# Attentions of a decoder layer: the product by the inverse one quarter earlier on VectorE, the layernorm scale behind a mask on GpSimd, the split of the output weights at a group's end

## The reference

```
x = x + attention(layernorm(x))                       # causal, 16 heads of 32
x = x + cross_attention(layernorm(x), ctx, ctx, mask) # keys and values of ctx, padding masked
x = x + experts(layernorm(x))                         # the one expert with the highest probability of 8
```

## Time and profile before

| | us |
|---|---|
| median of 3 runs | 2038.52 |
| lowest, highest | 2037.73, 2043.76 |
| profiled execution: its time | 2036.4 |
| profiled execution: its span | 2034.7 |

### The profile page before, as it was taken

The page is one execution under the profiler, slowest core; times in us unless marked ns, Lnnn a source line. Parts: engine busy times, 40 slices in busy tenths (PEclk is TensorE's granted clock), DMA queues, the critical chain, the costliest instruction groups (busy, mean ns, idle before and its releaser), DMA issues. The chain is left out here.

```text
span 2034.7 us, 34889 instructions
## 1 busy us (share of the span) xinstructions
PE 1882.0 (92%) x10942; PEld 1325.2 (65%) x10942; DVE 1342.8 (66%) x2837; ACT 1140.2 (56%) x2179; POOL 1000.9 (49%) x1147
## 2 busy tenths in 40 slices
PE   2999999999999999999999999999999835999997
PEld 2666666767666766656666666666666324898896
DVE  3666676666667676767575757575765335688886
ACT  3455554555555465655565655565655515787885
POOL 3354555455545555445444545555554434345454
PEclk9999999999999999999999999999999967899999
DMA  6444545545454575445454544535443369322220
GB/s 202 105 101 110 123 103 131 120 107 135 109 132 100 124 182 125 110 113 125 105 125 105 119 111 111 119 87 127 91 103 79 74 201 333 121 78 88 79 86 21
DMA packets 138089, 239.96 MB, mean 118 GB/s; under 512 B 31114, under 2 KB 32434, under 8 KB 137872
## 3 DMA queue, kind: packets, MB, share of 16 engines
q1 hardware_dynamic: 105728, 191.00, 34.7%
q0 software_dynamic: 21968, 46.42, 11.6%
q10 hardware_dynamic: 10240, 0.64, 0.3%
HBM read 115.63 MB, written 50.02 MB: 81 GB/s over the span
## 5 line engine op out<-in xcount | busy, mean ns | idle before, releaser
L535 ACT ACTIVATE attn_probs<-attn_sT 128x512 f32<-128x512 f32 (+3 forms) x1024 | 529.1, 519 | 484.5 <-PE attn_sT L826 480.0
L442 POOL TENSOR_TENSOR attn_probs<-attn_probs 128x512 f32<-128x512 f32 (+2 forms) x384 | 531.1, 1401 | 177.0 <-PE attn_o_ps L841 125.7
L641 DVE TENSOR_REDUCE attn_m_col<-attn_sS 128x1 f32<-128x512 f32 x512 | 342.6, 687 | 193.9 <-PE attn_sS L810 186.1
L826 PE MATMUL attn_sT<-attn_stack 98*128 98x512 f32 (+2 forms) x1024 | 387.6, 390 | 2.8 <-ACT attn_probs L535 2.8
L810 PE MATMUL attn_sS<-attn_stack 97*128 97x512 f32 (+2 forms) x1024 | 369.3, 371 | 14.5 <-DVE attn_m_col L641 6.0
L647 DVE CUSTOM_DVE_ANT_0 attn_sS<-attn_sS,attn_cT_low 128x128 f32<-128x128 f32 x496 | 241.2, 504 | 191.1 <-PE attn_sS L810 187.5
L826 PEld LDWEIGHTS attn_sT<-attn_stack 98*128 98x128 f32 x1024 | 188.0, 189 | 210.1 <-ACT attn_probs L535 115.6
L430 POOL TENSOR_SCALAR_AFFINE_SELECT attn_probs<-attn_probs 128x256 f32<-128x256 f32 x256 | 132.0, 516 | 361.7 <-ACT attn_probs L535 361.6
L841 PE MATMUL attn_o_ps<-attn_probs,attn_V 128*32 128x512 f32 (+3 forms) x2048 | 233.5, 527 | 24.3 <-POOL attn_probs L430 19.6
L810 PEld LDWEIGHTS attn_sS<-attn_stack 97*128 97x128 f32 x1024 | 193.9, 190 | 70.1 <-DVE attn_m_col L641 18.3
L790 PE MATMUL attn_pj<-attn_xT_high,attn_w_high 128*128 128x512 f32 x384 | 153.1, 399 | 3.9 <-DVE attn_w_low L607 3.9
(11 more groups left out here) (190 smaller groups left out, 3765.0 us busy)
## 6 DMA issues: line engine op xcount, KB each, us to landing
attn_stack<-attn_stage SPq DMA_DIRECT2D x672, 128.0 KB, 2.3
attn_rows<-in_x_dram SPq DMA_DIRECT2D x64, 256.0 KB, 4.0
attn_rows<-x_after_self SPq DMA_DIRECT2D x64, 256.0 KB, 4.2
moe_w<-in_L_ffn_W_dram SPq DMA_DIRECT2D x16, 1024.0 KB, 14.9
attn_stack<-attn_stage POOLq DMA_DIRECT2D x96, 128.0 KB, 3.4
x_after_self<-attn_rows SPq DMA_DIRECT2D x32, 256.0 KB, 2.6
x_after_self<-in_L_attn_b_dense_dram POOLq DMA_DIRECT2D x32, 256.0 KB, 5.0
attn_rows<-in_ctx_dram SPq DMA_DIRECT2D x32, 256.0 KB, 3.0
```

Source lines behind the costliest of these rows:

```text
L442: pool.tensor_tensor(total, total, tile_of(n, kb)[:, js, q0:S], ALU.add).then_inc(added, 1)
L535: act.activation(tile_of(n, kb)[:, j, q0:S], sT[:, i % 2, q0:S], ACT.Exp, scale=SCALE).then_inc(exp_done, 1)
L641: dve.tensor_reduce(to, sS[:, k % 2], AX_X, ALU.max).then_inc(s_free, 1)
L826: pe.matmul(sT[:, i % 2, q0:S], stack[0:ROW_MAX + 1, n % 2, 1, j, kb * P:(kb + 1) * P], stack[0:ROW_MAX + 1, n % 2, 0, j, q0:S], start=Tru ...
```

## The change

Three edits, each of the order alone: no instruction is added or taken away.

1. VectorE issues `divide` at q = 2 and `residual_of_inverse` at q = 3, each in the other's place, in all 64 groups.
2. Where the next batch is one of the self-attention, GpSimd's `layernorm_scale` of the first two row blocks goes from (g, q) = (0, 14) to (0, 15), and so behind the mask of q = 15. There are seven such batches with a group before them (b + 1 = 1 to 7).
3. The output weights of the cross-attention are split from (35, 14) on, that is at (35, 14), (35, 15), (36, 0) and (36, 1) on ScalarE, in place of (35, 6) to (35, 9); on VectorE one step later each.

```
@@ def scaled
-        half = (... if crosses(b + 1) else {(0, 14): 0, (1, 0): 1}).get((g, q))
+        half = (... if crosses(b + 1) else {(0, 15): 0, (1, 0): 1}).get((g, q))
@@ swaps
-    swaps = [(1, FIRST_CROSS - 3, 9), (0, FIRST_CROSS - 3, 14), (2, FIRST_CROSS - 2, 6), (3, FIRST_CROSS + 3, 6)]
+    swaps = [(1, FIRST_CROSS - 3, 9), (0, FIRST_CROSS - 3, 14), (2, FIRST_CROSS - 2, 6), (3, FIRST_CROSS + 3, 14)]
@@ block.vector, the walk over (n, q)
                 if q == 2 and in_groups(n - 1):
+                    divide(n - 1)
+                if q == 3 and in_groups(n - 1):
                     residual_of_inverse(n - 1)
-                if q == 3 and in_groups(n - 1):
-                    divide(n - 1)
```

More of the change, by code:

```diff
@@ L108, in scaled @@
             return None
-        half = ({(0, 15): 0, (1, 11): 1} if crosses(b + 1) else {(0, 14): 0, (1, 0): 1}).get((g, q))
+        half = ({(0, 15): 0, (1, 11): 1} if crosses(b + 1) else {(0, 15): 0, (1, 0): 1}).get((g, q))
         return None if half is None or (b < 0 and half == 0) else (b + 1, half)
```

## The result

| | median, us | lowest to highest | runs |
|---|---|---|---|
| before | 2038.12 | 2035.56 to 2043.76 | 4 |
| changed | 2014.76 | 2012.57 to 2016.20 | 4 |

The ratio is 0.9871, with a 95% interval of 0.9843 to 0.9900: 23.4 us less between the medians. The profiled execution took 2012.57 us with a span of 2010.8 (before 2036.4 and 2034.7), 23.8 us less.

What follows compares the result with a forecast made beforehand. TensorE, busy for 92% of the span, was taken to bound the kernel. Savings of 10.4 + 7.5 + 5.9 = 23.8 us were to bring the median from 2038.5 to 2014.7 us, range 2010 to 2022.

Steps and rivals of the forecast that it cites:

- Edit 1, 10.4: Self-attention, q = 4: mask of q = 3 no longer held up by VectorE's product, 29 TensorE waits of 0.36 us gone.
- rival A: Mask of q = 3: the residual holds it up as the product did, so nothing is won there; 2025.1 us, chance 0.10.
- Edit 2, 7.5: Between g = 0 and g = 1: mask ahead of the layernorm scale, all seven TensorE waits gone, 7.5 us; bounds 7.0 and 8.2.
- the list of the seven waits: Between g = 0 and g = 1: waits of 0.73 to 1.15 us, four of 1.12 between first and last, together 7.5.
- Edit 3, 5.9: Group 35: subtractions no longer beside GpSimd's additions, TensorE's 2.30 us wait and lower clock gone, 5.9 us.
- leaves TensorE no wait: Start of group 36: VectorE's maxima come 0.5 to 0.9 us late, but scores run two maxima ahead, so TensorE never stands.
- if a wait for a maximum ... stands in group 36: Group 36: a wait for a maximum or a lower clock there would show the output-weights term of 5.9 us wrong.
- Rival B: Group 36: the moved split costs a 0.9 us wait and 3.1 us of lower clock; 2018.7 us, chance 0.10.
- The sum: Whole kernel: 10.4 + 7.5 + 5.9 = 23.8 us less, profiled execution 2036.4 to 2012.6, median 2038.5 to 2014.7.
- Rival C: Self-attention: waits return at the next maximum or exponent; if all 17.9 us come back, 2032.6 us, chance 0.04.
- Rival D: Self-attention: without pauses TensorE's clock falls; over a tenth of 700 us it costs 35, giving 2050; chance 0.03.

Runs made afterwards that it cites:

- edit 3 alone: The kernel before with only the split of the output weights moved from (35, 6) to (35, 14): 2033.6 us against 2037.8, ratio 0.9987.

## Why the prediction was right

The forecast was 23.8 us; 23.4 and 23.8 were measured. By its terms:

- *Edit 1, 10.4.* Right in mechanism and size: 10.6 us over 28 groups, 11.0 for 29. It lies between the wait that the trace showed and the 0.40 by which the mask got shorter, both of which the range held. The bound of 0, rival A, fell with the first mask of 0.41 beside line 661.
- *Edit 2, 7.5.* Right: 7.3 us for six waits, so about 8 with the first, between the two bounds. It is 1.2 for each and not 1.1, since the product can start a little before the matmul ahead of it is done (607.98, where that one ends at 608.05), which the idle time doesn't count. In the list of the seven waits the prediction has one of 1.12 too many between the first and the last: there are three, and the sum of 7.5 is right.
- *Edit 3, 5.9.* The mechanism was right and the term too large: 4.8. The step that failed is the walk which "leaves TensorE no wait". Two scores are due at q = 3, so two before those of q = 4 is the first of q = 3, and its maximum was 0.74 us late. By its own sign ("if a wait for a maximum ... stands in group 36") the prediction was wrong here. Rival B had the delay (it allowed 0.9 us), but not the lower clock that it feared. With the split at q = 12 the whole 5.9 is there: 31.3 to 25.4.
- *The sum.* The terms as measured come to 11.0 + 8.0 + 4.8 = 23.8. In the changed kernel all three together gave about 0.9 us less inside groups 1 to 29 than edits 1 and 2 did apart (17.0 against 17.9), of which one wait of 0.36 us for a DMA is seen. What is left over nearly cancels: the start (+2.0, or +3.1 without the two waits that were won in it), the lower clock that the kernel before had in group 1 (about -1.9), the last groups (+1.0) and the expert stage (-3.2), together -1.0 (23.8 - 0.9 + 1.0 = 23.9, the difference of the spans). That the total hit so well is in part luck: any of these moves by more than 2 us from run to run.
- *Rival C* was not far. VectorE's room is 0.66 us, before the maximum of q = 5 and not of q = 4 as the prediction has it; the run with the product at q = 4 overdrew it by 0.43 in each group and lost 15 us on balance.
- *Rival D*: TensorE at 99% for 600 us was granted 1.00.

## What to carry to other kernels

A short operation that takes twice its time beside another engine's is worth finding: go from the wait to its releaser, and from there to what runs beside it at that moment. Moving a VectorE operation with two SBUF inputs by one slot, to where GpSimd has nothing that is waited for, won 11 us at no cost; but the slot has to have room for what is queued behind, or more is lost than was won. And on an engine that issues in order, work that nobody needs soon goes behind the work that the bounding engine waits for, not a quarter of a group later but behind it.

## What the runs showed of the hardware that was not expected

- The hold-up is all or nothing, in both directions: whether the mask began 0.14 or 0.45 us into the product, it ended 0.95 us after the product's start; and VectorE's subtraction and its line 678 both ended 0.55 us behind GpSimd's addition.
- A standing of TensorE of 2.3 us in group 35 was followed by the lower clock, and both went together. Behind none of the six waits of 1.12 to 1.15 us between g = 0 and g = 1 in the kernel before was it granted. In group 1 three waits of about 1.09, 0.28 and 0.79 us lie within 4 us in all eleven traces; the lower clock followed in three of them (3.4, 3.4 and 6.8 us) and not in the others. In the last group, with many short waits, the lower level was granted in some runs and not in others, for up to 20 us. This fits the scatter of the times: of the twelve runs of edit 3 alone, eight took 2030.3 to 2033.9 us at a mean granted clock of 0.976 to 0.979, four took 2038.7 to 2040.0 at 0.973.
- Two VectorE operations in a row, the second waiting for the first's result, cost 0.79 us from start to start in place of 0.60 (lines 666 and 671, in the run with the product at q = 4).
